# Second part of a convolution and window-attention kernel: a new order of operations on every engine, a fixed PSUM bank for each product, a semaphore for each operation, and probabilities read 49 columns at a time

## The reference

```python
def _vit(t, ...):                       # t: windows, 49 tokens, 96 channels
    h = _ln(t, ln1_s, ln1_b)
    q = (h @ wq + bq).reshape(N, S, 12, 8)
    k = (h @ wk + bk).reshape(N, S, 12, 8)
    v = (h @ wv + bv).reshape(N, S, 12, 8)
    scores = jnp.einsum('nqhd,nkhd->nhqk', q, k) / np.sqrt(8)
    attn = jax.nn.softmax(scores, axis=-1)
    o = jnp.einsum('nhqk,nkhd->nqhd', attn, v).reshape(N, S, D)
    t = t + o @ wo + bo
    h = _ln(t, ln2_s, ln2_b)
    return t + jax.nn.gelu(h @ w1 + b1) @ w2 + b2
x = x + conv(_gn(x))
x = x + windows(_gn(x))                 # roll, cut, _vit, put together, roll back
```

## Time and profile before

| what | value |
|---|---|
| median of 3 runs | 5549.4 us (5547.65 to 5557.69) |
| the profiled execution, whole | 5562.92 us |
| its span | 5561.1 us |
| busy TensorE matmul, VectorE, ScalarE, GpSimd | 94%, 63%, 63%, 59% of the span |
| mean granted TensorE clock | 0.973 |

### The profile page before, as it was taken

The page is one execution under the profiler, slowest core; times in us unless marked ns, Lnnn a source line. Parts: engine busy times, 40 slices in busy tenths (PEclk is TensorE's granted clock), DMA queues, the critical chain, the costliest instruction groups (busy, mean ns, idle before and its releaser), DMA issues.

```text
span 5561.1 us, 226903 instructions
## 1 busy us (share of the span) xinstructions
PE 5255.0 (94%) x96016; PEld 4120.8 (74%) x96016; DVE 3480.8 (63%) x5850; ACT 3529.1 (63%) x5398; POOL 3275.6 (59%) x4463
## 2 busy tenths in 40 slices
PE   7999999996899999999999999999999999999998
PEld 7999999996666666666666666666666666666665
DVE  4444444443567776776767676777766767776673
ACT  4444444443577777776777776777776777777674
POOL 1000000002577777777777777777777777777774
PEclk9999999998699999999999999999999999999996
DMA  6455554542666666666666666666666666666662
GB/s 165 122 130 132 125 141 122 137 122 60 132 139 139 140 140 141 139 140 132 140 138 142 140 140 133 138 140 139 142 141 132 142 140 140 139 139 142 133 140 46
DMA packets 1154820, 740.27 MB, mean 133 GB/s; under 512 B 452852, under 2 KB 1141076, under 8 KB 1153716
## 3 DMA queue, kind: packets, MB, share of 16 engines
q1 hardware_dynamic: 1153812, 725.76, 58.6%
HBM read 409.02 MB, written 316.46 MB: 130 GB/s over the span
## 4 chain that ended last, share of the span: by engine, by line
PE 63%; issue 7%; DVE 3%; ACT 3%; POOL 0%; ACTq 0%; DVEq 0%; POOLq 0%
PE ps_pv L1069 14%; PE ps_ring L1136 8%; PE ps_s L1023 5%; PE ps_ring L1006 4%; PE ps_xc L1111 4%; PE ps_ring L997 4%; PE ps_t L1023 4%; PE ps_ring L1128 4%; PE ps_ring L1014 4%; PE ps_ring L1008 3%; PE ps_ring L1007 3%; DVE b_rest L931 2%; ACT b_sq_hi L796 2%; PE ps_ring L1097 2%; PE ps_ring L1015 2%
## 5 line engine op out<-in xcount | busy, mean ns | idle before, releaser
L888 DVE TENSOR_REDUCE b_mx<-ps_s 113x12 f32<-113x588 f32 x1024 | 783.8, 765 | 205.0 <-PE ps_s L1023 204.6
L1069 PEld LDWEIGHTS ps_pv<-b_vd,b_probs_t 128*64 128x64 f32 x24576 | 775.6, 140 | 164.2 <-issue 155.1
L788 ACT ACTIVATE b_probs_t<-ps_t 128x588 f32<-128x588 f32 x1024 | 667.6, 652 | 307.6 <-PE ps_t L1023 307.6
L1069 PE MATMUL ps_pv<-b_vd,b_probs_t 128*64 128x18 f32 x24576 | 826.8, 214 | 0.0
L694 POOL TENSOR_TENSOR b_mid_lo<-b_mid,b_mid_hi 128x392 fp32r<-128x392 f32 x768 | 789.2, 1028 | 43.3
L225 POOL TENSOR_SCALAR xn<-xin,aff 128x2016 f32<-128x2016 f32 x64 | 93.4, 1470 | 1152.4 <-DVE aff L332 1152.4
L749 POOL TENSOR_TENSOR b_outs<-b_y,b_xs 96x392 f32<-96x392 f32 x256 | 316.8, 1237 | 443.5 <-DVE b_y L969 443.5
L803 ACT ACTIVATE b_mid<-ps_ring,b_cols 128x392 f32<-128x392 f32 x768 | 438.5, 587 | 202.0 <-PE ps_ring L1008 186.3
L775 ACT ACTIVATE b_lg<-ps_ring,b_cols 96x392 f32<-96x392 f32 x512 | 298.4, 583 | 325.7 <-PE ps_ring L1015 322.7
L736 POOL TENSOR_SCALAR b_planes<-b_rest 96x784 bf16<-96x784 f32 x256 | 215.5, 842 | 452.2 <-DVE b_rest L935 452.2
L291 DVE TENSOR_TENSOR xt_lo<-xt,xt_hi 128x896 fp32r<-128x896 f32 x96 | 104.8, 1092 | 602.2 <-ACT xt_hi L254 602.2
(11 more groups left out here) (133 smaller groups left out, 12014.8 us busy)
## 6 DMA issues: line engine op xcount, KB each, us to landing
stacked_qk<-b_planes SPq DMA_DIRECT2D x512, 220.5 KB, 2.9
b_q_st<-stacked_qk SPq DMA_DIRECT2D x512, 220.5 KB, 4.3
b_k_st<-stacked_qk SPq DMA_DIRECT2D x512, 220.5 KB, 5.7
toep<-filters_padded SPq DMA_DIRECT2D x96, 936.5 KB, 7.0
stacked_qk<-b_planes SPq DMA_DIRECT2D x512, 147.0 KB, 2.4
stacked_qk<-b_planes SPq DMA_DIRECT2D x512, 73.5 KB, 1.9
b_xs<-x_scratch SPq DMA_DIRECT2D x224, 147.0 KB, 2.8
out<-b_outs SPq DMA_DIRECT2D x224, 147.0 KB, 3.2
```

The source lines that it names most:

```text
L788: act.activation(pt[:, p, 0:HEADS * TOK].rearrange("k (e n) -> k e n", e=2), ps_t[:, :, 0:HPAIR * TOK], ACT.Exp, scale=float(DH) ** -0.5). ...
L888: dve.tensor_reduce(mx[0:rows_q, :].rearrange("q (e m p) -> q e m p", e=2, p=PAIRS)[:, :, :, p], ps_s[0:rows_q, :, 0:HPAIR * TOK].rearrang ...
L1069: ins = pe.matmul(to, pt[:, p, at:at + WS], vd[:, m % VR, p, h, :, :], start=True, stop=True, skip_group_check=True)
```

## The change

`DEPTH` periods are added behind the 256 strips as before. On each engine the operations get a new order and new distances. `strip(t, b)` is strip t - b in period t, or nothing at either end; each engine counts its own periods, so only the order on one engine and the differences of b on it have a meaning. Each product gets a fixed bank: `BANKS` lists the users of each bank in the order in which TensorE takes them, with the semaphores that free it, and `wait_bank` waits for the user before. Semaphores that counted all four groups or all three MLP parts become one for each, so some operations wait for more of them. `rstd` becomes two tiles. `probs_t` is 15 columns shorter and the pv products load 49 columns of it as weights. The arithmetic is unchanged. The stack loads are split: `load_k` of strip n stays ahead of the `put`s of strip n+1, `load_q` of strip n comes behind planes 0 and 1 of strip n+1. The five functions `step` stand below in the order SyncE, GpSimd, ScalarE, VectorE, TensorE.

```diff
     B = NWIN
-    LOAD, GN, QKV, STK, ATT, MAXR, SOFT, PROJ, MLPS, STORE = 0, 1, 2, 3, 4, 5, 6, 7, 8, 9
+    NSTRIP = BATCH * B
+    DEPTH = 9
     VR, XS, SR = 6, 10, 4
     NMAX = HEADS * PAIRS
     MAXAT = 296
+    BANKS = {
+        "r0": (
+            ("q", 2, ("q_done",)),
+            ("var2", 7, ("lg2",)),
+            ("w2", 8, ("y_done",)),
+            ("w1_0", 7, ("gelu0",)),
+            ("ot", 6, ("ot_done",)),
+        ),
+        "r1": (
+            ("wo", 7, ("t1_done",)),
+            ("k", 2, ("k_done",)),
+            ("v", 2, ("v_done",)),
+            ("w1_1", 7, ("gelu1",)),
+            ("w1_2", 7, ("gelu2",)),
+            ("var1", 1, ("lg1",)),
+        ),
+        "x": (
+            ("xc2", 7, ("h2_high", "h2_done",)),
+            ("xc1", 1, ("h1_done",)),
+        ),
+    }
...
-        pt = sb("probs_t", [P, PAIRS, HEADS * TOK + WS - TOK])
+        pt = sb("probs_t", [P, PAIRS, HEADS * TOK])
...
+            def load_stack(n, side, dst):
+                all_planes_written(sp, n)
+                after(sp, "r_ps3", n - SR)
+                rows_e = stk[n % 2, side].rearrange("(m r) j t -> (r j) m t", m=HPAIR)
+                for e in range(2):
+                    sp.dma_start(dst[WS * e:WS * e + SLOT, n % SR, :, :],
+                                 rows_e[SLOT * e:SLOT * e + SLOT]).then_inc(stk_loaded[n % 2], 16)
...
+            def step(t):
+                n = strip(t, 0)
+                if n is not None:
+                    load(n)
+                n = strip(t, 9)
+                if n is not None:
+                    store(n)
+                n = strip(t, 3)
+                if n is not None:
+                    load_k(n)
+                n = strip(t, 5)
+                if n is not None:
+                    maxima_in(n)
+                n = strip(t, 2)
+                if n is not None:
+                    put(n, 0, ("q_high", "k_high"))
+                    put(n, 1, ("rest_high",))
+                n = strip(t, 3)
+                if n is not None:
+                    load_q(n)
+                n = strip(t, 4)
+                if n is not None:
+                    maxima_out(n)
+                n = strip(t, 2)
+                if n is not None:
+                    put(n, 2, ("qk_split",))
+            steps(step)
...
+            def step(t):
+                n = strip(t, 8)
+                if n is not None:
+                    mid_low(n, 1)
+                    mid_low(n, 0)
+                n = strip(t, 1)
+                if n is not None:
+                    tokens_high(n)
+                n = strip(t, 2)
+                if n is not None:
+                    plane_mid(n)
+                    plane_low(n)
+                n = strip(t, 1)
+                if n is not None:
+                    tokens_low(n)
+                n = strip(t, 0)
+                if n is not None:
+                    wrap_in(n)
+                n = strip(t, 8)
+                if n is not None:
+                    add_out(n)
+                n = strip(t, 4)
+                if n is not None:
+                    max_mid(n)
+                    max_low(n)
+                n = strip(t, 1)
+                if n is not None:
+                    square_low(n)
+                n = strip(t, 7)
+                if n is not None:
+                    mid_high(n, 0)
+                    mid_high(n, 2)
+                n = strip(t, 8)
+                if n is not None:
+                    wrap_out(n)
+                n = strip(t, 0)
+                if n is not None:
+                    tokens_in(n)
+                n = strip(t, 7)
+                if n is not None:
+                    mid_high(n, 1)
+                    mid_low(n, 2)
+            steps(step)
...
+            def step(t):
+                n = strip(t, 3)
+                if n is not None:
+                    high_plane(n, 0, "q", "q_high")
+                n = strip(t, 8)
+                if n is not None:
+                    square(n, sq2_hi, "xc2", "sq2_high", 1.0, ("sq2_split", "var2"))
+                    square(n, sq2, "xc2", "sq2", 1.0, ("sq2_split",))
+                n = strip(t, 3)
+                if n is not None:
+                    high_plane(n, 1, "k", "k_high")
+                n = strip(t, 6)
+                if n is not None:
+                    exps(n, 0)
+                n = strip(t, 8)
+                if n is not None:
+                    log_var(n, "var2", "lg2")
+                    inv_std(n, rstd2, "lg2", "rstd2", ("h2_high", "h2_done"))
+                n = strip(t, 6)
+                if n is not None:
+                    exps(n, 1)
+                if strip(t, 8) is not None:
+                    act.preload_act_table_set("gelu_apprx_tanh_and_others")
+                n = strip(t, 8)
+                if n is not None:
+                    gelu(n, 1)
+                n = strip(t, 2)
+                if n is not None:
+                    square(n, sq1_hi, "xc1", "sq1_high", 1.0 / C, ("sq1_split", "var1"))
+                    square(n, sq1, "xc1", "sq1", 1.0 / C, ("sq1_split",))
+                n = strip(t, 8)
+                if n is not None:
+                    gelu(n, 0)
+                    gelu(n, 2)
+                if strip(t, 8) is not None:
+                    act.preload_act_table_set("natural_log_exp_and_others")
+                n = strip(t, 2)
+                if n is not None:
+                    log_var(n, "var1", "lg1")
+                    inv_std(n, rstd1, "lg1", "rstd1", ("h1_done",))
+                n = strip(t, 6)
+                if n is not None:
+                    exps(n, 2)
+                    exps(n, 3)
+            steps(step)
...
+            def step(t):
+                n = strip(t, 2)
+                if n is not None:
+                    plane_rest(n, 1, "k", "k_high", "k_done")
+                n = strip(t, 6)
+                if n is not None:
+                    row_sum(n)
+                n = strip(t, 4)
+                if n is not None:
+                    max_high(n)
+                    max_rest(n)
+                n = strip(t, 2)
+                if n is not None:
+                    value_blocks(n)
+                n = strip(t, 7)
+                if n is not None:
+                    norm2(n)
+                    norm2_high(n)
+                n = strip(t, 8)
+                if n is not None:
+                    mlp_out(n)
+                n = strip(t, 7)
+                if n is not None:
+                    norm2_low(n)
+                n = strip(t, 3)
+                if n is not None:
+                    row_max(n, 0)
+                n = strip(t, 6)
+                if n is not None:
+                    normalise(n)
+                n = strip(t, 3)
+                if n is not None:
+                    row_max(n, 1)
+                    row_max(n, 2)
+                n = strip(t, 6)
+                if n is not None:
+                    turned_o(n)
+                n = strip(t, 1)
+                if n is not None:
+                    norm1(n)
+                n = strip(t, 6)
+                if n is not None:
+                    attended(n)
+                n = strip(t, 1)
+                if n is not None:
+                    plane_rest(n, 0, "q", "q_high", "q_done")
+                n = strip(t, 3)
+                if n is not None:
+                    row_max(n, 3)
+                n = strip(t, 6)
+                if n is not None:
+                    square_low(n)
+            steps(step)
...
+            def step(t):
+                n = strip(t, 7)
+                if n is not None:
+                    project(n)
+                n = strip(t, 4)
+                if n is not None:
+                    scores(n, 3)
+                n = strip(t, 6)
+                if n is not None:
+                    below_max(n, 3)
+                n = strip(t, 2)
+                if n is not None:
+                    query_key(n, 0, "q")
+                n = strip(t, 7)
+                if n is not None:
+                    centre_sum(n)
+                n = strip(t, 2)
+                if n is not None:
+                    query_key(n, 1, "k")
+                n = strip(t, 6)
+                if n is not None:
+                    times_v(n, 1)
+                n = strip(t, 5)
+                if n is not None:
+                    below_max(n, 0)
+                n = strip(t, 4)
+                if n is not None:
+                    max_rows(n)
+                n = strip(t, 7)
+                if n is not None:
+                    spread(n, "var2", sq2_hi, sq2_lo, "sq2_split")
+                n = strip(t, 2)
+                if n is not None:
+                    value(n)
+                n = strip(t, 5)
+                if n is not None:
+                    below_max(n, 1)
+                n = strip(t, 8)
+                if n is not None:
+                    contract(n)
+                n = strip(t, 3)
```

(45 more changed lines are left out.)

759 lines of the change are left out of this document (328 added, 431 removed).

## The result

The changed kernel takes 7004.4 us in the middle of four runs (6952.5 to 7097.5), the kernel before beside it 5553.6: a ratio of 1.258, interval 1.252 to 1.263. From the turns of the maxima (now L1199, from 1407.8 to 7022.1 us) there are 255 distances of 22.02 us each, and 1481.4 us for everything else; before they were 15.99 and 1484.5. The whole loss, 1534.6 us of span, is therefore in the step.

A forecast was written before the change was run, and what follows sets the result against it. The prediction took the late load_q loop, with TensorE's clock halved by its wait, to bound the step at 22.5 us: 1484.5 + 255 x 22.5 = 7222, plus 1.8, minus 13.5, 7210 us; own range 6830 to 7850, widened to 6000 to 7850.

The forecast's parts named there:

- part three: Loop s0, k, plane 1, its put, load_q, next s0: 18.1 us at full clock, TensorE idle 3.4 us ahead of s0.
- Before, s0 came a period later and this tie did not exist: In the kernel before, s0 was said to stand a period later, so put and load_q closed no loop.
- The other ties fit into such a step: Waits besides load_q's stay hidden in 18.1 us; the maxima land some 2 us before r0 needs them.
- hardly any other idle time: Sign of being right: TensorE idles ahead of s0 once a step, released by the q stack's DMA, and hardly elsewhere.
- The signs on the clock: Sign of being right: granted clock well under 0.97, about 0.6 to 0.75, changing every step or two.
- TensorE is therefore the bound: Kernel before: TensorE has 15.1 us of work in each 15.9 us step and one wait of 0.80 us.
- loads in time: Rival: load_q lands within 2 us, the h2_low wait ahead of w1_1 decides; step 15.9, 5527 us; chance 0.05.
- Neither loop binds: Rival: an operation was misplaced by a period, TensorE bound at 14.7 us a step, 5221 us; chance 0.03.
- part two: TensorE's new order: 0.2 us more for one more lone group, making its work 14.7 us a step.
- part one: pv's weight loads of 49 columns instead of 64: 0.6 us less TensorE work a strip.
- part four: The wait ahead of s0 halves TensorE's clock, work slows by 1.7; steps average between 21.2 and 25.0, taken 22.5 us.
- clock stays up: Rival: TensorE keeps 2.4 GHz for most steps, the loop alone gives 18.1 us, 6090 us; chance 0.24.

The follow-up runs named there:

- e10: The fastest repaired kernel (q loads and maxima early, h2_low ahead of y, centre_tokens ahead of w1_1) with only load_q put back behind the next strip's puts: 7008.2 us (1.259).
- e5: The kernel before with only SyncE's q stack loads moved behind the puts of planes 0 and 1 of the next strip: 8147.6 us (1.467).
- e1: The changed kernel with only load_q moved ahead of load_k of the same strip, so ahead of the next strip's puts: 7055.6 us (1.268).
- e4: The changed kernel with 20 needless products on TensorE ahead of s0's wait for the stack loads: 6348.5 us (1.142).
- e3: The kernel before with only pv's weight loads cut to 49 columns of the probabilities instead of 64: 5504.6 us (0.989).
- e7: The changed kernel with load_q early, h2_low ahead of y, and the maxima early on GpSimd and SyncE: 5534.6 us (0.994).
- e8: e7 with centre_tokens ahead of w1_1 on TensorE, and w1's products with the high plane no longer waiting for the low one: 5381.9 us (0.967).
- e9: e8 with the probabilities loaded in 64 columns again instead of 49: 5481.1 us (0.985).
- e6: The changed kernel with only the maxima early (split ahead of add_out on GpSimd, loaded right behind their store on SyncE), load_q left late: 7146.7 us (1.287).

## Why the prediction was right, point by point

- **The loop (part three): right, in its length and in its pieces.** From k's start to the next s0 the forecast had 18.1 - 8.7 = 9.4 us; the timeline has 3005.93 - 2996.57 = 9.36. k_high starts 0.97 later (forecast 1.0), the rest ends at 2.26 (2.5), plane 1 at 3.25 (3.5), the first of the two loads is issued at 4.5 (the second forecast at 5.0), and s0 comes 4.8 after it. From s0 to k it had 8.7 and took 9.12, of which 0.59 is the wait ahead of w1_1. The whole is 18.5 us for 18.1, and 18.2 where nothing else of the change is there (e10). e5 and e10 show that this loop is enough by itself.
- **Its reason was wrong in one place.** "Before, s0 came a period later and this tie did not exist": s0 stands as close behind k there (5.8 us, 3009.09 - 3003.3), and e5 shows the tie as soon as the loads are late. What had kept it away was SyncE's order alone, with the loads ahead of the next put.
- **"The other ties fit into such a step": wrong in its size.** The maxima were said to land some 2 us ahead of r0. They have nothing to spare: their loop is some 18.3 us long at full clock (e1, and the waits ahead of r0 in e4), as long as the forecast's own, and 20.5 us where its wait throws the clock back (e1). In the changed kernel it showed little (11.3 of 1000 us), because most steps are longer. The step that failed was taking the maxima's path from its operations, without what is queued ahead of them: add_out waiting for y on GpSimd (5.84 us), nine DMAs on SyncE, and 5.7 us from the load's issue to r0, behind the four stack loads. The loop through w2, y, h2_low and w1_1, called hidden, showed too: 21.1 of 1000 us. So the sign "hardly any other idle time" failed: of 81 idle microseconds in the stretch 47.8 stand ahead of s0. The signs on the clock (0.66) and on the landing held; that ScalarE, VectorE and GpSimd would be busy for less than half of the time held for VectorE (48%), while the other two had 52% and 54%.
- **"TensorE is therefore the bound" (the reading of the kernel before): wrong for the usual step.** e3 took 0.6 us of work out and left that step at 15.8 us. The forecast does not rest on it, since it adds up the work and not the old step.
- **The rival "loads in time" would have failed for the same reason.** It gave 5527 us; e1, which is that case, took 7056. Its own price was fair: 1.2 us of stall for h2 behind y, 0.9 in e1. Only e7 comes near its time, and by chance: it has h2 first, so that the rival's stall is not in it, and gets there with a usual step of 15.2 us and 25 long ones.
- **"Neither loop binds", 5221 us:** the work of part two was right, 14.7 us for 15.03 - 0.40 = 14.6 in e8, but the step of 14.7 that the rival makes of it was reached by no kernel: e8, the nearest, takes 5382, with 0.4 us of waiting and 0.3 us of irregular steps in the mean.
- **The 49 columns (part one): right.** 0.6 us of work a step; a pv takes 1.21 us for the 1.2 forecast, and e9 gives 0.54 for the two. The Trainium skill (TensorE: Matmul & The Clock Gate, LDWEIGHTS) would have 12.5 ns for 15 columns. Half of that (the half is the forecast's estimate) for 96 records is 0.6, and the measured 0.54 to 0.60 agrees. Only the difference does: by that rule a whole load of 64 columns would be 53 ns, and its row has 138. What it is worth depends on what ends next: 0.03 us in the usual step and 0.20 in the mean of the old order (e3), 0.54 and 0.41 in e8's.
- **The clock (part four): right in kind, nearly in size.** The mean step was 22.02 us for 22.5, between long steps of 23 to 26 (forecast 24.3 to 25.0) and short ones of 17 to 19.5 (18.1). The 22.5 was a choice between 21.2 and 25.0, so that it comes this near is luck in part. The stretches at half clock have a median of 20.5 us, for the 20 taken. The forecast's alternation is not the whole picture either: from s0 to s0, 26 steps that ran for about half of their time at 1.2 GHz still ended in a wait of 3.6 us. The factor 1.7 was near: a pv takes 2.12 us at 1.2 GHz and 1.21 at 2.4, 1.75. The fall at 1337 us, which the prediction sets beside a DMA wait, came in a wait of 8 us for VectorE (`sums1c`, L347); a fall behind a wait for a DMA is first seen in the changed kernel, behind the 3.14 us ahead of s0. e4 shows the clock's part by itself, with more work and 656 us less. The time was 206 us below the forecast: 123 of these are the step's 0.48 us in the profiled run, 3 the rest of its span, and 80 are that I took the profiled run to lie 13.5 us above the median; here it lay 93 us above it.
- **The rival "clock stays up"** (6090 us) got what e4 forces: 6349. Without needless work the clock doesn't stay up, so its 0.24 was too much for a wait of 3 us in one piece.

## What to carry to other kernels

When one queue carries several transfers for each period, write down for each loop what stands ahead of its transfer in that queue: moving two loads behind the next strip's put cost 1626 us of 5382 (e10), though the path of the transfer, and not the work of any engine, was what grew. Two loops of nearly the same length, here some 18.5 us, hide each other; opening one shows nothing (e1, e6), so look at which wait appears in its place before the theory is dropped. The length of a loop is read at full clock: the 20.5 us of e1 are some 18.3 and the clock's fall. A wait that comes back in every step is paid twice, once in time and once in the clock, and it can be worth filling (e4, e8).

## What the runs showed of the hardware

- The maxima's load, issued right behind the four stack loads, let r0 start only 5.7 us later in e1; the q stack's loads of the changed kernel took 4.3 us to land.
- The idle time in a step doesn't decide by itself whether the clock falls for long. All of TensorE's idle time in the stretch, for each step, against the steps over 20 us of 255: e3 1.30 us and 1 step, e7 0.87 us and 25, before 0.80 us and 6, e8 0.64 us and 5. In e7 the wait stands ahead of w1, before and in e3 ahead of var2. What does decide was not settled.
- Each fall costs more than its wait: the 53 steps over 16.5 us of e7 lie together 220 us above the usual 15.2, for 32 falls some 7 us each, where the wait of a step is 0.7 us.
- A pv of 48 records at 1.2 GHz takes 2.12 us with 49 columns (changed kernel) and 2.68 with 64 (e5), at 2.4 GHz 1.21 and 1.51.
